# Three products of a two-layer transformer kernel moved on the tensor engine's queue

## The chip, the cores and the metric

The kernel runs on one NeuronCore of a Trainium2 chip. Its engines have a queue of instructions each and meet only through semaphores: TensorE (PE, matmuls and transposes), VectorE (DVE), ScalarE (ACT), GpSimd (POOL) and SyncE (SP, which here issues every DMA). The metric is the device time of one execution in microseconds (us). Before the change it was 1876.63 us, the median of 3 runs (1875.66 to 1876.63).

## The reference

Four sequences of 512 tokens by 256 features pass two layers. Shortened to what is computed:

```python
x = L0_attn_x                                  # (4, 512, 256)
xn = _layernorm(x)
x = x + attn(xn) + ffn0(xn)    # 16 heads of 128, causal; a binarized 256x256 product with bias
xn = _layernorm(x)
x = x + mamba2(xn) + ffn1(xn)  # 64 heads of 64 (32 pairs), state 128; a gated product of width 704

# attn, for each head: k, q, v = W_K xn, W_Q xn, W_V xn
scores = q k^T, masked, softmax;  z = attn v;  out = W_O z
# mamba2: proj = xn @ in_proj_w (a gate, x, B, C and dt), a convolution of 4 taps and silu on x, B and C,
# the state-space product in chunks, times silu(gate), an RMS norm over 4096, out_proj_w
```

## The kernel before, in words

The order of the work on each engine is written out by hand, one function per engine. `sequence(b, last)` is one of the four sequences, b = 0 to 3. It runs 16 attention heads (`head`), the end of the attention, the start of the second layer, and then 32 pairs of Mamba heads (`pair`, numbered n = 0 to 31).

Where more than plain fp32 rounding is wanted, an operand is split in a high part (ACT copies it out of PSUM as fp32r) and a low part (DVE or POOL subtracts the high one), and three matmuls are made of one (`mm3`, line 745). So a projection of queries or of keys over 256 features is 6 matmuls of 128x512, and a half of the values is 12 of 128x256.

**A head.** On PE: the queries (into bank 0) and keys (bank 1) of the next head (`project_qk`), the transposes of this head's probabilities (`turn_probs`, lines 831, 837 and 842), for even heads the second half of the values of this head and the next one (`project_v`, bank 0), the scores of the next head (`score`, from line 750), and probabilities times values (`weigh_values`). DVE takes in this order: the low parts of the next queries (line 1455) and keys (line 1426), three low parts of the turned probabilities, the low part of the values, the mask and the maxima, and `normalise` (line 1499), which divides the next head's probabilities by their sum. ACT copies the high parts in the same order: queries, keys, three of probabilities, values.

`project_v` overwrites bank 0 and so waits for `s_q_ev`, which line 1455 counts up when the queries have left it. `turn_probs` waits for `s_norm_done` from line 1499. `weigh_values` waits for `s_v_ev`, the low part of the values. The first head of the first sequence has its queries, keys, first half of values, scores and `normalise` ahead of the loop.

**A pair.** On PE: the gate of pair n+1 (`project_gate`, bank 0), the x of pair n+2 (`project_x`, bank 1), the transposes of the x of pair n+1 (`turn_x`, line 1006, which waits for the convolution's end on DVE, line 1519), the output product of pair n-1 (`project_out`, line 1047, which waits for DVE line 1687), and then `in_block` (L1034), `off_block` (L1023) and `make_states` (L1014). Pair 30 has no `project_x`, since there is no pair 32. Pair 31 makes the queries and keys of the next sequence's head 0 (`first_qk`), reading that sequence's normalised input from its own place, `xn_next`. After pair 31 come the first half of the next sequence's values (`project_v`), its first scores, `project_out` of pair 31, and a sum of squares (line 1129).

**Weights.** There are two buffers, `w_r` of parity 0 and 1. In the first sequence they are loaded, split and saved to DRAM; afterwards SP fetches the split ones. SP's queue at the end of a sequence is `next_heads(b, par)`: for parity 0 it waits until the gate of pair 30 has been made (the last reader of that buffer), and fetches head 0's query and key weights (line 415) and value weights (line 418). For parity 1 it waits for the gate of pair 31, copies `xn_next` to `xn_r` (line 435), and fetches head 1's weights. In the first sequence the saves and loads of the output weights (lines 412 and 400) stand ahead of both, and SP takes its queue strictly in order. `w_wait` is PE's wait for such a fetch (semaphore `w_fetched0` for parity 0).

Of the kernel before, what the change touches and what calls it, by code (L numbers as in the profile page):

```python
# [34 lines left out]
def two_layers(nc, x, wqkv, wo_t, w0, b0, w_pair, w_out, w_bc, w_dt, conv_par, dt_bias, a_log,  # L35
               d_col, norm_col, gate_t, up_t, down_t, gate_s, up_s, down_s, out):
    NB, S, D = x.shape
    NH = wqkv.shape[0]
# [16 lines left out]
    with ExitStack() as ctx:  # L55
# [268 lines left out]
        def first(b):  # L324

            return isinstance(b, int) and b == 0
# [410 lines left out]
        def _(pe):  # L737
# [49 lines left out]
            def project_qk(b, h, par, lows=None, src=xn_now):  # L787
                N = b * NH + h
                w_wait(b, h, par)
                pe.wait_ge(s_v_ev, N + 1 - par)  # L790
                project(bank[0][:], par, 0, lows, src).then_inc(s_q_done, 1)
                pe.wait_ge(s_k_ev, N + 1)
                project(bank[1][:], par, 1, src=src).then_inc(s_k_done, 1)
# [28 lines left out]
            def turn_probs(b, h, par):  # L822
                N = b * NH + h
                pe.wait_ge(s_norm_done, N + 1)
                if not first(b):
                    pe.wait_ge(s_ms_ready, b)
                pe.wait_ge(s_pt_a, N + 1)
                if par == 0:
                    pe.wait_ge(s_v_ev, N + 2)
                for q in range(NT):  # L830
                    ins = pe.transpose(bank[5][:, q * P:(q + 1) * P], prob[:, par, P_AT[q]:P_AT[q] + P], ident[:])  # L831
                ins.then_inc(s_turned_a, 1)
                pe.wait_ge(s_pt_b, N + 1)
                pe.wait_ge(s_y_done, b * 2 + 1)
                for k, q in ((1, 1), (1, 2), (1, 3), (3, 3)):
                    at = PT_AT[k] - PT_AT[1] + (q - k) * P
                    ins = pe.transpose(bank[6][:, at:at + P], prob[:, par, P_AT[q] + k * P:P_AT[q] + (k + 1) * P], ident[:])  # L837
                ins.then_inc(s_turned_b, 1)
                pe.wait_ge(s_z_ev, N + 1)
                pe.wait_ge(s_y_done, b * 2 + 2)  # L840
                for q in (2, 3):
                    ins = pe.transpose(bank[7][:, (q - 2) * P:(q - 1) * P], prob[:, par, P_AT[q] + 2 * P:P_AT[q] + 3 * P], ident[:])
                ins.then_inc(s_turned_c, 1)
# [148 lines left out]
            def project_x(b, n, par):  # L992
                N = b * NPAIR + n
                w_wait(b, NH + n, par)
                pe.wait_ge(s_taps_done, N + b * 2 + 2)
                project(bank[1][:], par, 1).then_inc(s_xc_done, 1)
# [51 lines left out]
                             start=begin and t % 2 == 0, stop=last, skip_group_check=True)  # L1048
                ins.then_inc(s_projected, 1)

            def first_qk(b):

                project_qk(b, 0, 0, lows=b * 2 * KT, src=xn_now if first(b) else xn_next)

            def sequence(b, last):
                def head(h, par, more):

                    if more:
                        project_qk(b, h + 1, 1 - par)
                    turn_probs(b, h, par)  # L1060
                    if par == 0:
                        project_v(b, h + 1, 1, 0)
                    if more:
                        score(b, h + 1, 1 - par)
                    weigh_values(b, h, par)
                    if more and par == 1:
                        project_v(b, h + 1, 0, 5)

                with pe.Fori(0, NH // 2 - 1) as i:
                    for par in range(2):  # L1070
                        head(i * 2 + par, par, True)
                head(NH - 2, 0, True)
                pe.wait_ge(s_late, 16 * N_LATE)

                pe.wait_ge(s_v_ev, (b + 1) * NH + 1)
                pe.wait_ge(s_z_ev, (b + 1) * NH - 1)
                out_heads(0, range(NH - 2))
                turn_probs(b, NH - 1, 1)
                pe.wait_ge(s_k_ev, (b + 1) * NH + 1)
                out_heads(1, range(NH - 2))  # L1080
                weigh_values(b, NH - 1, 1)
                attention_out(b)

                mamba_start(b, last)

                def pair(n, par, more, ahead, before=2):


                    if more:
                        project_gate(b, n + 1, 1 - par)  # L1090
                    elif not last:
                        pe.wait_ge(s_gate_ready, (b + 1) * NPAIR + 1)
                        pe.wait_ge(s_taps_done, (b + 1) * (NPAIR + 2))
                        first_qk(b + 1)
                    if ahead:
                        project_x(b, n + 2, par)
                    if more:
                        turn_x(b, n + 1, 1 - par)
                    if before == 1:
                        pe.wait_ge(s_res_ready, b + 1)  # L1100
                    if before > 0:
                        project_out(b, n - 1, 1 - par, isinstance(n, int) and n == 1, False)
                    in_block(b, n, par)
                    off_block(b, n, par)
                    if more:
                        make_states(b, n + 1, 1 - par)

                make_states(b, 0, 0)
                pair(0, 0, True, True, before=0)
                pair(1, 1, True, True, before=1)  # L1110
                with pe.Fori(1, NPAIR // 2 - 1) as i:
                    for par in range(2):
                        pair(i * 2 + par, par, True, True)
                pair(NPAIR - 2, 0, True, False)
                pair(NPAIR - 1, 1, False, False)
                if not last:
                    pe.wait_ge(s_xn_copied, (b + 1) * 64)
                    project_v(b + 1, 0, 0, 0)
                if not last:
                    pe.wait_ge(s_state_ev, (b + 1) * NPAIR + 1)  # L1120
                    score(b + 1, 0, 0)
                    pe.wait_ge(s_v_ev, (b + 1) * NH + 2)
                project_out(b, NPAIR - 1, 1, False, True)
                pe.wait_ge(s_summed, (b + 1) * (NPAIR + 1) - (1 if last else 0))
                pe.wait_ge(s_hid_ready, (b + 1) * NPAIR + 1)
                if last:
                    pe.wait_ge(s_squared, (b + 1) * NPAIR + 1)
                for t in range(NT):
                    ins = mm(bank[5][:, t:t + 1], lhsT=sumsq[:, t * P:(t + 1) * P], rhs=ones[:, 0:1], start=True, stop=not last)
                    if last:  # L1130
                        ins = mm(bank[5][:, t:t + 1], lhsT=square[:, t * P:(t + 1) * P], rhs=ones[:, 0:1], start=False, stop=True)
                ins.then_inc(s_ss_done, 1)
# [1 line left out]
            keep_busy(11)  # L1134
            turn_norm(0, range(NT), (6, 7)).then_inc(s_ln_turned, 1)
            keep_busy(8)
            first_qk(0)
            project_v(0, 0, 0, 0)
            score(0, 0, 0)
            pe.wait_ge(s_v_ev, 2)  # L1140
# [669 lines left out]
```

## Time and profile before

| | |
|---|---|
| median of 3 runs | 1876.63 us (1875.66 to 1876.63) |
| the profiled execution | 1876.75 us |
| its span | 1875.0 us |
| PE busy | 1852.3 us, 99% |
| DVE, ACT, POOL busy | 1500.1, 1237.9, 828.0 us |
| mean granted clock of TensorE | 0.999 |

The 1.75 us between span and time lie outside the recorded instructions. The span is one row of four sequences: the first head's scores begin at about 18 us, and the second, third and fourth sequences' first queries and keys at 473.87, 936.50 and 1398.50 us. In a row of a timeline, a group of instructions has its start and the busy time from there. Matmuls overlap (the next begins before the modelled end of the last), so the room that a group takes on PE is read from its start to the start of the next one, not from its busy time.

### The profile page before, as it was taken

The page shows a single profiled execution, that of the slowest core. Times are in us where ns is not written, and L with a number is a line of the kernel's source. Part 1 is how long each engine was busy: PE and PEld are TensorE (multiplying, and loading weights), DVE is VectorE, ACT ScalarE, POOL GpSimd, SP SyncE. Part 2 cuts the span into 40 slices and gives each one's busy share as a digit, 9 for nine tenths or more (in the row PEclk, how much of TensorE's full clock was granted, in tenths as well). Part 3 has the DMA queues.
Part 4 walks back from the last instruction along what each step waited for, and adds up shares of the span by engine and source line. Part 5 has one row for each costly group of instructions (what it writes and reads, how often), then busy time and mean ns, then how long its engine had stood idle before and what let it go on. Part 6 is the DMA issues. An engine that isn't in the chain of part 4 may idle for free.

```text
span 1875.0 us, 42153 instructions
## 1 busy us (share of the span) xinstructions
PE 1852.3 (99%) x12602; PEld 1574.3 (84%) x12602; DVE 1500.1 (80%) x2736; ACT 1237.9 (66%) x2867; POOL 828.0 (44%) x1005
## 2 busy tenths in 40 slices
PE   8999999999999999999999999999999999999998
PEld 7888778888888878888888887888888888788886
DVE  6886778888788468888888846988888883688886
ACT  5663489999455247888755525888865551588885
POOL 2210379998200027777710002777770000277776
PEclk9999999999999999999999999999999999999999
DMA  6330478887422125656622212656652321366663
GB/s 242 126 126 1 158 231 264 259 265 240 144 78 89 54 82 194 209 205 218 210 98 79 77 54 82 227 205 206 217 189 90 91 66 54 117 215 205 207 215 112
DMA packets 157193, 290.76 MB, mean 155 GB/s; under 512 B 12944, under 2 KB 83792, under 8 KB 157008
## 3 DMA queue, kind: packets, MB, share of 16 engines
q1 hardware_dynamic: 157136, 290.04, 46.6%
q8 instruction: 31, 0.51, 0.1%
q14 instruction: 26, 0.21, 0.0%
HBM read 248.70 MB, written 38.14 MB: 153 GB/s over the span
## 4 chain that ended last, share of the span: by engine, by line
PE 92%; DVE 3%; ACT 2%; issue 1%; POOL 1%; DMA 0%; SPq 0%; POOLq 0%; DVEq 0%; ACTq 0%
PE bank L745 40%; PE bank L1047 11%; PE bank L1034 7%; PE bank L1014 6%; PE both L745 5%; PE bank L863 4%; PE bank L1023 4%; PE bank L1006 3%; PE bank L912 2%; PE bank L831 1%; PE bank L837 1%; PE both L863 1%; PE bank L753 1%; PE bank L750 1%; PE bank L751 1%
## 5 line engine op out<-in xcount | busy, mean ns | idle before, releaser
L745 PE MATMUL bank<-xn_r,w_r 128*128 128x512 f32 x2268 | 566.6, 398 | 0.9 <-DVE xn_r L1738 0.9
L745 PEld LDWEIGHTS bank<-xn_r,w_r 128*128 128x128 f32 x2268 | 412.6, 188 | 83.6 <-issue 1.1
L1510 DVE SCALAR_TENSOR_TENSOR conv_acc<-bank,conv_sb,conv_acc 128x511 f32<-128x511 f32 (+2 forms) x408 | 304.0, 745 | 44.7 <-DVE conv_acc L1510 17.3
L605 POOL TENSOR_TENSOR rstd<-var_eps,minus_half 128x4 f32<-128x4 f32 (+2 forms) x12 | 9.7, 807 | 603.8 <-DVE var_eps L1439 603.8
L1047 PE MATMUL bank<-wo_n,place 128*128 128x256 f32 x1024 | 242.4, 380 | 2.3 <-DVE place L1687 2.3
L626 POOL TENSOR_TENSOR c_grow<-c_grow,c_t 128x768 f32<-128x768 f32 x128 | 234.0, 1828 | 22.5 <-DVE place L1519 22.5
L1159 ACT ACTIVATE place_r<-bank 128x512 fp32r<-128x512 f32 (+1 forms) x320 | 158.7, 556 | 120.6 <-PE bank L745 96.0
L1426 DVE TENSOR_TENSOR place_r<-bank,place_r 128x512 fp32r<-128x512 f32 (+1 forms) x320 | 186.3, 630 | 63.6 <-ACT place_r L1159 63.6
L1047 PEld LDWEIGHTS bank<-wo_n,place 128*128 128x128 f32 x1024 | 184.8, 190 | 22.8 <-DVE place L1687 2.7
L648 POOL TENSOR_TENSOR sumsq<-sumsq,place 128x512 f32<-128x512 f32 x127 | 162.0, 1276 | 17.0 <-ACT place L1227 17.0
L1238 ACT ACTIVATE conv_acc<-bank,conv_sb 128x512 f32<-128x512 f32 x136 | 105.7, 778 | 89.2 <-PE bank L745 85.3
L636 POOL TENSOR_TENSOR carry<-state,dec 128x128 f32<-128x128 f32 x256 | 102.5, 400 | 133.9 <-ACT state L1154 112.7
L1344 ACT ACTIVATE place<-place_r,cum_t 128x128 f32<-128x128 f32 x512 | 156.0, 389 | 0.0
L1344 ACT ACTIVATE span_b<-place_r,cum_t 128x128 f32<-128x128 f32 x512 | 155.9, 389 | 0.0
L1536 DVE TENSOR_TENSOR shared<-both,cb 128x1024 f32<-128x1024 f32 x128 | 155.4, 1214 | 0.0
L1034 PEld LDWEIGHTS bank<-shared,place 128*64 128x64 f32 x2048 | 109.2, 136 | 41.8 <-issue 41.1
L619 POOL TENSOR_TENSOR shared<-place,dec 128x384 f32<-128x384 f32 x128 | 106.5, 832 | 82.6 <-DVE place L1543 82.5
L1034 PE MATMUL bank<-shared,place 128*64 128x128 f32 x2048 | 140.1, 279 | 0.0
L745 PE MATMUL bank<-place_r 128*128 128x512 f32 (+3 forms) x768 | 133.1, 322 | 0.5
L1519 DVE SCALAR_TENSOR_TENSOR place<-bank,conv_acc 128x512 f32<-128x512 f32 x128 | 88.4, 691 | 54.6 <-ACT bank L1243 54.4
L745 PEld LDWEIGHTS bank<-place_r 128*128 128x128 f32 x768 | 120.1, 188 | 14.0 <-issue 5.5
L641 POOL TENSOR_TENSOR state<-state,carry 128x128 f32<-128x128 f32 x256 | 118.4, 462 | 20.1
(174 smaller groups left out, 3544.8 us busy)
## 6 DMA issues: line engine op xcount, KB each, us to landing
place_r<-cum_rows SPq DMA_DIRECT2D x128, 512.0 KB, 4.3
c_grow<-grow_rows SPq DMA_DIRECT2D x128, 384.0 KB, 3.5
w_r<-pair_split SPq DMA_DIRECT2D x96, 512.0 KB, 3.7
w_r<-qkv_split SPq DMA_DIRECT2D x48, 512.0 KB, 4.0
pair_split<-w_r SPq DMA_DIRECT2D x32, 512.0 KB, 3.4
qkv_split<-w_r SPq DMA_DIRECT2D x16, 768.0 KB, 3.9
w_r<-qkv_split SPq DMA_DIRECT2D x48, 256.0 KB, 3.2
wo_n<-out_split SPq DMA_DIRECT2D x96, 128.0 KB, 2.0
```

Source lines behind the costliest of these rows:

```text
L626: pool.tensor_tensor(c_grow[:, par, :, :], c_grow[:, par, :, :], c_t[:, P:W].unsqueeze(1).to_broadcast([P, 2, W - P]), ALU.mult).then_inc( ...
L641: pool.tensor_tensor(state[:, c, :], state[:, c, :], carry[:], ALU.add).then_inc(s_carried, 1)
L648: pool.tensor_tensor(sumsq[:], sumsq[:], square, ALU.add).then_inc(s_summed, 1)
L745: ins = mm(out, lhsT=w(a), rhs=m(b), start=(start and i == 0), stop=(stop and i == 2), **kw)
L1014: ins = mm(bank[2][:, c * P:(c + 1) * P], lhsT=b_sb[:, c, :], rhs=x_w[:, c, :], start=True, stop=True)
L1034: ins = mm(bank[5][h * HD:(h + 1) * HD, c * P:(c + 1) * P], lhsT=x_dt[:, par, c, h * HD:(h + 1) * HD], rhs=mix[:, par, h, c * P:(c + 1) * ...
L1047: ins = mm(out_tile((6, 7), t), lhsT=hid[:, t * P:(t + 1) * P], rhs=wo_n[:, par, :], start=begin and t % 2 == 0, stop=last, skip_group_che ...
L1159: A(dst, src, ACT.Copy).then_inc(done, 1)
L1344: ins = A(span[par][:, h, c * P:(c + 1) * P], spread[:, par, h * W + c * P:h * W + (c + 1) * P], ACT.Relu, bias=cum_t[:, c, bass.ds(n * 2 ...
L1426: tt(dst, src, high.bitcast(F32), ALU.subtract).then_inc(done, 1)
L1510: stt(out=conv_acc[:, back:W], in0=src[:, 0:W - back], scalar=conv_sb[:, ch, TAPS - 1 - back:TAPS - back], in1=conv_acc[:, back:W], op0=AL ...
L1536: tt(mix[:, par, :, :], both[:].rearrange("p (h w) -> p h w", h=2), cb[:].rearrange("p t i -> p (t i)").unsqueeze(1).to_broadcast([P, 2, W ...
```

## The change

On PE alone, at three places; no other engine's program is touched. In the first sequence's head 0, `project_v` stands ahead of `turn_probs`. At the end of sequences 0 to 2, `first_qk` is taken apart: the keys (`first_k`, with the waits for the weights, for `xn_next` and for bank 1) go to pair 30, to where `project_x` stands in other pairs, and the queries (`first_q`) stay in pair 31. And heads 0 and 1 of every sequence are written out ahead of the loop over heads, which begins at head 2.

```diff
-            def first_qk(b):
-
-                project_qk(b, 0, 0, lows=b * 2 * KT, src=xn_now if first(b) else xn_next)
+            def first_q(b):
+                pe.wait_ge(s_v_ev, b * NH + 1)
+                project(bank[0][:], 0, 0, src=xn_next).then_inc(s_q_done, 1)
+
+            def first_k(b):
+                w_wait(b, 0, 0)
+                pe.wait_ge(s_k_ev, b * NH + 1)
+                project(bank[1][:], 0, 1, b * 2 * KT, xn_next).then_inc(s_k_done, 1)
 
             def sequence(b, last):
-                def head(h, par, more):
+                def head(h, par, more, begin=False):
 
                     if more:
                         project_qk(b, h + 1, 1 - par)
+                    if begin:
+                        project_v(b, h + 1, 1, 0)
                     turn_probs(b, h, par)
-                    if par == 0:
+                    if par == 0 and not begin:
                         project_v(b, h + 1, 1, 0)
...
-                with pe.Fori(0, NH // 2 - 1) as i:
+                for h in range(2):
+                    head(h, h, True, begin=first(b) and h == 0)
+                with pe.Fori(1, NH // 2 - 1) as i:
...
                         pe.wait_ge(s_gate_ready, (b + 1) * NPAIR + 1)
-                        pe.wait_ge(s_taps_done, (b + 1) * (NPAIR + 2))
-                        first_qk(b + 1)
+                        first_q(b + 1)
                     if ahead:
                         project_x(b, n + 2, par)
+                    elif more and not last:
+                        pe.wait_ge(s_taps_done, (b + 1) * (NPAIR + 2))
+                        first_k(b + 1)
...
-            first_qk(0)
+            project_qk(0, 0, 0, lows=0)
```

PE's queue in the first sequence's head 0, before (`place_r,w_r` and `xn_r,w_r` are products of the input with query or key weights, `w_r,xn_r` is half of the values, `ident,place` are transposes; a loop's entry comes first):

```order
L1069 UNCONDITIONAL_BRANCH [waits v_ev]
L1069 ISA
L790 REGISTER_ALU [waits w_ready]
L745 MATMUL bank<-xn_r,w_r 128x512 [waits v_ev]
L745 MATMUL bank<-xn_r,w_r 128x512 x5
L792 REGISTER_ALU
L745 MATMUL bank<-xn_r,w_r 128x512 [waits k_ev]
L745 MATMUL bank<-xn_r,w_r 128x512 x5
L831 MATMUL bank<-ident,place 128x128 [waits v_ev,pt_a,norm_done]
```

The same place after the change:

```order
L745 MATMUL bank<-xn_r,w_r 128x512 [waits v_ev,w_ready]
L745 MATMUL bank<-xn_r,w_r 128x512 x5
L745 MATMUL bank<-xn_r,w_r 128x512 [waits k_ev]
L745 MATMUL bank<-xn_r,w_r 128x512 x5
L745 MATMUL bank<-w_r,xn_r 128x256 [waits q_ev,w_ready]
L745 MATMUL bank<-w_r,xn_r 128x256 x11
L831 MATMUL bank<-ident,place 128x128 [waits v_ev,pt_a,norm_done]
```

The twelve matmuls of the values, with their wait for `q_ev`, have come ahead of the transposes and their wait for `norm_done`.

PE's queue in pair 30 and at the head of pair 31 of the first sequence, before:

```order
L745 MATMUL bank<-xn_r,w_r 128x512 [waits gate_ready]
L745 MATMUL bank<-xn_r,w_r 128x512 x5
L1006 MATMUL bank<-ident,place 128x128 [waits conv_silu]
...
L1014 MATMUL bank<-shared,b_sb 128x128 x2
L745 MATMUL bank<-place_r,w_r 128x512 [waits v_ev,w_fetched0,xn_lo,taps_done,gate_ready]
L745 MATMUL bank<-place_r,w_r 128x512 x2
L745 MATMUL bank<-place_r,w_r 128x512 [waits xn_lo]
L745 MATMUL bank<-place_r,w_r 128x512 x2
L745 MATMUL bank<-place_r,w_r 128x512 [waits k_ev]
L745 MATMUL bank<-place_r,w_r 128x512 x5
```

The same place after the change:

```order
L745 MATMUL bank<-xn_r,w_r 128x512 [waits gate_ready]
L745 MATMUL bank<-xn_r,w_r 128x512 x5
L745 MATMUL bank<-place_r,w_r 128x512 [waits k_ev,xn_lo,w_fetched0,taps_done]
L745 MATMUL bank<-place_r,w_r 128x512 x2
L745 MATMUL bank<-place_r,w_r 128x512 [waits xn_lo]
L745 MATMUL bank<-place_r,w_r 128x512 x2
L1006 MATMUL bank<-ident,place 128x128 [waits conv_silu]
...
L1014 MATMUL bank<-shared,b_sb 128x128 x2
L745 MATMUL bank<-place_r,w_r 128x512 [waits v_ev,gate_ready]
L745 MATMUL bank<-place_r,w_r 128x512 x5
```

Six matmuls, and with them the waits for `w_fetched0` and `taps_done`, have moved from behind pair 30's work to right behind the gate of pair 31.

## Rows read from the trace of the kernel before

**Rows 1.** The page: busy time of each engine.
```profile
PE 1852.3 (99%) x12602; PEld 1574.3 (84%) x12602; DVE 1500.1 (80%) x2736; ACT 1237.9 (66%) x2867; POOL 828.0 (44%) x1005
```
**Rows 2.** Waits of PE: total us, times, longest us.
```profile
PE bank L1006 <- DVE place L1519: 2.3, 5, 0.5
```
**Rows 3.** Timeline of PE, first heads: start us, busy us, group, idle before.
```profile
19.85 2.95 PE L745 MATMUL bank<-xn_r,w_r 128*128 128x512 f32 x12
24.51 0.66 PE L831 MATMUL bank<-ident,place 128*128 128x128 f32 x4 [1.72 <-DVE place L1499]
...
25.58 1.67 PE L745 MATMUL bank<-w_r,xn_r 128*128 128x256 f32 x12
27.09 0.40 PE L750 MATMUL bank<-place_r 128*128 128x512 f32 x1
...
29.02 2.04 PE L745 MATMUL bank<-place_r 128*128 128x512 f32 x12
...
33.71 0.63 PE L831 MATMUL bank<-ident,place 128*128 128x128 f32 x4
```
**Rows 4.** Timeline of DVE, the same stretch.
```profile
23.18 1.27 DVE L1499 TENSOR_SCALAR place<-place,inv_total 128x128 f32<-128x128 f32 x4
24.37 0.68 DVE L1455 SCALAR_TENSOR_TENSOR place_r<-bank,place_r 128x512 fp32r<-128x512 f32 x1
...
25.89 1.62 DVE L1426 TENSOR_TENSOR place_r<-bank,place_r 128x512 fp32r<-128x512 f32 x3 [0.24 <-ACT place_r L1159]
27.92 0.69 DVE L1426 TENSOR_TENSOR place_r<-bank,place_r 128x512 fp32r<-128x512 f32 x1 [0.41 <-ACT place_r L1159]
...
32.35 1.27 DVE L1499 TENSOR_SCALAR place<-place,inv_total 128x128 f32<-128x128 f32 x4
```
**Rows 5.** Timeline of PE, end of the first sequence.
```profile
466.48 1.64 PE L745 MATMUL bank<-xn_r,w_r 128*128 128x512 f32 x6
468.67 0.65 PE L1006 MATMUL bank<-ident,place 128*128 128x128 f32 x4 [0.55 <-DVE place L1519]
...
473.87 3.03 PE L745 MATMUL bank<-place_r,w_r 128*128 128x512 f32 x12 [0.27 <-issue]
476.74 1.89 PE L1047 MATMUL bank<-wo_n,place 128*128 128x256 f32 x8
...
480.94 1.67 PE L745 MATMUL bank<-w_r,xn_r 128*128 128x256 f32 x12 [0.64 <-DMA w_r<-qkv_split]
```
**Rows 6.** SP's queue there; and DMA issues of 467.3 to 468: KB, us to landing.
```profile
467.46 0.63 SPq L415 DMA_DIRECT2D w_r<-qkv_split  x1
...
w_r<-qkv_split SPq DMA_DIRECT2D x1, 512.0 KB, 6.2
```
**Rows 7.** Timeline of PE, end of the second sequence.
```profile
929.62 1.64 PE L745 MATMUL bank<-xn_r,w_r 128*128 128x512 f32 x6
931.81 0.66 PE L1006 MATMUL bank<-ident,place 128*128 128x128 f32 x4 [0.55 <-DVE place L1519]
...
939.40 1.89 PE L1047 MATMUL bank<-wo_n,place 128*128 128x256 f32 x8
...
942.89 1.70 PE L745 MATMUL bank<-w_r,xn_r 128*128 128x256 f32 x12
```
**Rows 8.** Timeline of DVE, the same stretch.
```profile
936.72 0.69 DVE L1687 TENSOR_TENSOR place<-bank,place 128x512 f32<-128x512 f32 x1
```
**Rows 9.** DMA issues of 923.7 to 924.4: KB, us to landing.
```profile
w_r<-qkv_split SPq DMA_DIRECT2D x1, 512.0 KB, 3.9
```
**Rows 10.** Timeline of PE's start; two stretches behind its last matmul (PEclk third from right).
```profile
3.57 4.65 PE L759 MATMUL both<-upto,ident 128*128 128x128 f32 x22 [3.57 <-POOL causal_bf L599]
...
10.44 1.95 PE L759 MATMUL both<-upto,ident 128*128 128x128 f32 x16
...
1869.41:1871.68 2.27, 0.00 (x0) 0.00 (x0) 1.04 (x4) 0.00 (x0) 1.02 (x1) 0.92 0.00 0
...
1871.40:1873.00 1.60, 0.00 (x0) 0.00 (x0) 1.06 (x3) 0.00 (x0) 0.00 (x0) 0.50 0.23 84
```

## The prediction

> **What bounds the kernel.** I read the page's busy times first: PE is busy 99% of the span [rows 1], so a change on PE's queue can give back only the idle time it removes, and every wait it adds is paid in full unless a later wait of PE shrinks by it. Next the waits of PE over the whole run. The one that the moved keys aim at comes 5 times with 2.3 us in total, once in pair 30 of each sequence [rows 2]. Then the timelines of PE, DVE and SP at the two places of the change, to see what each moved instruction waits for at its new place. About 0.2% (3.75 us) is what a measurement of this kernel can tell from no change.
>
> **Term A, the first head.** Before, PE has issued the queries and keys of head 1 by about 22.8 (19.85 + 2.95) and stands still until 24.51, when `normalise` (23.18 + 1.27 = 24.45) lets the transposes go [rows 3, 4]. The values are put in front of that wait. But they overwrite bank 0, and wait for the queries to leave it, and that is line 1455, which stands behind `normalise` in DVE's queue and ends at 24.37 + 0.68 = 25.05 [rows 4]. So the values cannot begin before about 25.15: the wait becomes longer by 0.6 us instead of being filled. From there:
> - The values take 27.09 - 25.58 = 1.51 us of PE [rows 3] and end at 26.7. The transposes, which began at 24.51, begin at 26.7, 2.2 later.
> - DVE's three low parts of the probabilities began 1.38 behind the transposes (25.89 against 24.51) and its low part of the values ended 2.72 behind that beginning (27.92 + 0.69 = 28.61) [rows 3, 4]. ACT and DVE take the probabilities first and then the values, so the early values gain nothing there; with no pause between them (the two idles of 0.24 and 0.41 in rows 4 mostly go) the four take about 2.2, and end near 26.7 + 1.38 + 2.2 = 30.25. Before it was 28.61: 1.65 later.
> - `weigh_values` needs that last one. It began at 29.02 without a wait [rows 3] and will begin at about 30.35. The mask, maxima, exponentials and second `normalise` hang on DVE's queue in the same way: that one ended at 32.35 + 1.27 = 33.62, and PE's transposes began at 33.71 with 0.09 to spare [rows 3, 4]. At 33.62 + 1.65 = 35.27 it releases them at 35.3.
> That is +1.6 us at 33.71. From there PE has no wait behind which it could hide. The bounds: +0.6 if only the wait for bank 0 is paid and the ones behind it vanish, +2.2 if the whole shift of the transposes stays. I take +1.6, since the row of the second `normalise` sets it.
>
> **Term B, the end of the first sequence.** The gate of pair 31 begins at 466.48. Twelve matmuls of this shape take 476.74 - 473.87 = 2.87 us of PE, so six take 1.43, and PE is free at 467.9 [rows 5]. Before, it stood until the transposes at 468.67. Now the keys come here, and with them the wait for head 0's weights. SP issues that fetch at 467.46, and it lands 6.2 us later, at 473.66 [rows 6]. Before, the first product that read it began at 473.87 [rows 5], right behind that landing; it was already late there, since from the transposes to that product it took 5.20 us here (473.87 - 468.67) and 4.72 in the second sequence (939.40 - 2.87 - 931.81) [rows 5, 7]. SP cannot issue it sooner: nothing on SP depends on the moved matmuls, and what stands ahead of it is unchanged. So PE waits with `turn_x`, `project_out`, `in_block`, `off_block` and `make_states` of pair 30 queued behind the keys, from 467.9 to 473.87.
> - `turn_x` begins at 473.87 + 1.43 = 475.3. From `turn_x` to the values of the next sequence the second sequence took 942.89 - 931.81 = 11.08 us [rows 7], of which 1.43, the keys, are now ahead: 9.65. The values begin at 484.95.
> - Before they began at 480.94, which holds a wait of 0.64 for head 1's weights [rows 5]; that wait is gone in the shift.
> B = +4.0 us. Bounds: the same fetch took 3.9 us at the second sequence [rows 9], which would put the keys at about 471.5 and B at +1.6; if it came as much later again as it here came behind that one (2.3 us), B would be +6.3. I take the landing of this very fetch.
>
> **Term C, the ends of the second and third sequences.** There nothing is saved or loaded by SP ahead of the fetch, it is issued before 924.4 and lands 3.9 us later [rows 9], well before PE needs it at 929.62 + 1.43 = 931.05 [rows 7]. The keys fill the gap until 931.81: `turn_x` begins at 932.48, 0.67 late, and the queries alone follow in pair 31, so `project_out` comes at 939.40 + 0.67 - 1.43 = 938.64. It needs line 1687, which ended at 937.41 and moves to 938.1 [rows 7, 8], so this wait does not come up. The gain is 0.76 each, -1.5 for two. Bounds 0 (a new wait of the same size) and -1.7.
>
> **Term D, the clock.** The longest wait of PE at the two places before is 1.72 us [rows 3], and the clock was full all along. Under this change it stands 6 us in B. The row that shows what this does is at the end: in the 2.27 us behind the last matmul the mean granted clock is 0.92, and from 1871.40 on it is 0.50 [rows 10], the lower of the two levels, 1.2 GHz against 2.4. So it fell after about 1.9 us of standing still (0.92 means 0.36 us of the 2.27 at half). At the start, PE's first 22 small matmuls took 4.65 us, 211 ns each, and 16 of the same a little later 1.95, 122 each [rows 10]; the difference over the 22 is 2.0 us. I take this as the price of one climb back after the 6 us: D = +2.0. Bounds 0 (the clock stays) and +4.0 (twice that).
> The Trainium skill, "TensorE: Matmul & The Clock Gate", section "HAM oscillation — how this bites in real kernels", says that a DMA wait between groups of matmuls can drop the clock, so that the next group starts at the lower one. The rows at the end of the span agree with it in kind; by this rule D is paid, and without it the sum is 2.0 less.
>
> **The two heads written out** (some 180 queue rows more) I cost at nothing: the stretch between the loops is already written out so, and PE has no wait for instructions there. The loop's edge costs nothing visible either. Bound: 0.5 us for a sequence, the size of the longest wait of rows 2.
>
> **Sum.** 1.6 + 4.0 - 1.5 + 2.0 = +6.1 on the span of 1875.0 is 1881.1; with the 1.75 outside it 1882.85. The profiled execution (1876.75) is 0.1 above the median (1876.63), so the forecast is 1882.7.
>
> **The rivals.**
> 1. *The clock stays up or recovers at once.* For it: the row at the end has small products ahead of the pause, where here large ones stand, and may not carry over. Against it: 6 us is three times the 1.9 after which it fell. D = 0: 1880.7. Chance 25%.
> 2. *The fetch lands sooner than in the trace before.* For it: 3.9 us at the second sequence [rows 9]. Against it: SP and the DMA traffic up to the landing are unchanged. B = 1.6 and a pause of 3.6 us; without D the sum is +1.7, 1878.4. Chance 10%. The Trainium skill, "DMA: Bandwidth & Descriptors", section "Anatomy of one DMA — SWDGE (gpsimd) path", gives about 2.0 us plus bytes over 436 GB/s for a DMA; for 512 KB that is an estimate of 3.2 us, against 6.2 measured here on another issuing path. By the page PE would stand some 3 us less in B.
> 3. *The keys are covered in all three ends, and the kernel is faster.* Place: the landing of that one fetch. The values would begin no later than before if it landed by 469.6 (480.94 - 9.65 - 1.43 and 0.2 for the start), 2.1 us after its issue; every tenth below is a gain. If it were there at 467.9, B would be -0.76 for the gap, -0.5 for the late start of 473.87 and -0.64 for the values' wait, -1.9, and the sum 1.6 - 1.9 - 1.5 = -1.8: 1874.8; with the queries out of bank 0 in time as well, A is about -1.5 and the time 1871.7. Against it stand both landings of rows 6 and 9. Chance 3%.
> 4. *It costs more*: the fetch lands later in the contended stretch, the clock takes two climbs, or the written-out heads cost instruction fetches. One of these at its bound gives about 1885. Chance 12%.
>
> The forecast keeps 50%. The range 1879.0 to 1885.5 takes in the rival without D, the forecast, and most of rival 4; some of 2 and 3 lie below. More than 0.2% slower is above 1880.4: the forecast, rival 4 and somewhat over half of rival 1, 0.76. Within 0.2%: the rest of rival 1 and rival 2, 0.20. Faster: 0.04.
>
> **What would show it.** In the profile after: the values of head 1 start at about 25.15, released by DVE L1455, and the second head's transposes near 35.3. One wait of PE near 6 us at 468 plus 1.6, released by the DMA `w_r<-qkv_split`; behind it matmuls of 512 columns at a longer spacing and a granted clock of 0.50 for some 4 us. In the next two ends no wait at L1006. If SP's fetch lands before 470, or the values start before 24.5, a step here is wrong.

## The result and the profile after

The change makes the kernel slower: 1885.68 us, the median of 5 runs (1882.13 to 1886.56), against 1876.62 us, the median of 5 runs of the kernel before (1875.66 to 1876.63). The ratio is 1.0047, with a 95% interval of 1.0032 to 1.0062. The forecast was 1882.7 in a range of 1879.0 to 1885.5 us, so the direction and the two waits hold, and the size was too small by 3 us: by the median the time is 0.2 us above the range's upper end, by the ratio (1.0047 on 1876.63 is 1885.45) right at it. It lies where the fourth rival, with a chance of 12%, had put it (about 1885). One execution in all the experiments, of the kernel of experiment 8, took 2295.31 us at a mean granted clock of 0.752, and no comparison here uses it.

The page and the waits of PE of the changed kernel (total us, times, longest us) answer to [rows 1, 2]:

```profile
PE 1856.7 (99%) x12602; PEld 1578.4 (84%) x12602; DVE 1499.7 (80%) x2736; ACT 1238.4 (66%) x2867; POOL 828.9 (44%) x1005
```

```profile
PE bank L745 <- issue: 5.9, 1, 5.9
...
PE bank L745 <- DVE place_r L1466: 3.0, 4, 2.4
...
PE bank L1006 <- DVE place L1530: 0.7, 2, 0.5
```

The same number of instructions keeps PE busy 4.4 us longer, which waits alone can't do. There is one wait of 5.9 us and one of 2.4, and the wait for the convolution's end has gone from 5 times to 2. The timeline of PE at the first head answers to [rows 3]:

```profile
20.41 2.92 PE L745 MATMUL bank<-xn_r,w_r 128*128 128x512 f32 x12
25.77 2.67 PE L745 MATMUL bank<-w_r,xn_r 128*128 128x256 f32 x12 [2.43 <-DVE place_r L1466]
28.24 1.05 PE L831 MATMUL bank<-ident,place 128*128 128x128 f32 x4
...
32.39 2.11 PE L745 MATMUL bank<-place_r 128*128 128x512 f32 x12 [0.38 <-DVE place_r L1437]
...
37.32 0.66 PE L831 MATMUL bank<-ident,place 128*128 128x128 f32 x4
```

The values wait for the queries' low part (line 1466 now), as forecast. But they then take 2.47 us of PE (28.24 - 25.77) where they took 1.51, and the transposes 1.05 where they took 0.66. The end of the first sequence answers to [rows 5]:

```profile
470.10 1.64 PE L745 MATMUL bank<-xn_r,w_r 128*128 128x512 f32 x6
477.60 2.90 PE L745 MATMUL bank<-place_r,w_r 128*128 128x512 f32 x6 [5.85 <-issue]
480.29 1.06 PE L1006 MATMUL bank<-ident,place 128*128 128x128 f32 x4
481.14 3.02 PE L1047 MATMUL bank<-wo_n,place 128*128 128x256 f32 x8
...
491.46 1.69 PE L745 MATMUL bank<-w_r,xn_r 128*128 128x256 f32 x12
```

Six matmuls of 512 columns take 2.69 us of PE (480.29 - 477.60) instead of 1.43, and the output product 2.95 (the next group began at 484.09) instead of 1.82. The stretches of both places (us, PE, PEld, DVE, ACT and POOL busy, granted clock, DMA share, GB/s) show why:

```profile
26.03:29.44 3.41, 3.41 (x18) 3.41 (x18) 0.19 (x1) 0.05 (x1) 1.44 (x1) 0.50 0.54 216
```

```profile
470.00:476.60 6.60, 1.75 (x10) 1.13 (x8) 3.39 (x5) 3.72 (x7) 2.94 (x5) 1.00 0.82 245
476.60:483.40 6.80, 5.80 (x16) 4.73 (x17) 0.69 (x1) 0.00 (x0) 1.24 (x2) 0.50 0.72 263
483.40:488.00 4.60, 4.60 (x45) 3.79 (x44) 2.08 (x3) 1.09 (x2) 1.97 (x3) 1.00 0.00 0
```

The granted clock was 0.50 (1.2 GHz) in both places, and not in the second one alone. The clock was still full until 476.60, about 4.9 us into the long wait. That wait is put down to "issue", which names no releaser; SP's queue in the changed kernel shows the fetch, issued 6.5 us before the keys began, and the list of DMA issues (KB, us to landing) shows it landing after 6.4:

```profile
470.55 0.43 SPq L400 DMA_DIRECT2D raw_out<-in_w_out  x1
471.09 0.63 SPq L415 DMA_DIRECT2D w_r<-qkv_split  x1
```

```profile
w_r<-qkv_split SPq DMA_DIRECT2D x1, 512.0 KB, 6.4
```

The end of the second sequence answers to [rows 7]:

```profile
940.16 1.64 PE L745 MATMUL bank<-xn_r,w_r 128*128 128x512 f32 x6
941.63 1.56 PE L745 MATMUL bank<-place_r,w_r 128*128 128x512 f32 x6
943.03 0.60 PE L1006 MATMUL bank<-ident,place 128*128 128x128 f32 x4
...
952.63 1.70 PE L745 MATMUL bank<-w_r,xn_r 128*128 128x256 f32 x12
```

Here nothing waits: from the gate to the values it is 12.47 us against 13.27 before (942.89 - 929.62), 0.80 less.

Measured from fixed points, the 8.9 us between the two spans (1883.9 and 1875.0) are all found:

| place | from start to start | before | after | difference |
|---|---|---|---|---|
| up to head 1's queries | 0 to PE L745 | 19.85 | 20.41 | +0.56 |
| first head | that to head 1's transposes | 13.86 | 16.91 | +3.05 |
| end of sequence 0 | gate of pair 31 to the values | 14.46 | 21.36 | +6.90 |
| end of sequence 1 | the same | 13.27 | 12.47 | -0.80 |
| end of sequence 2 | the same | 13.26 | 12.48 | -0.78 |

These are one profiled execution of each kernel, and not all of them are alike. Of the five executions of the changed kernel four took 1884.88 us or more, at mean granted clocks of 0.995 and 0.996, and one 1882.13 us, at 0.998. And the 14.46 us before, at the end of sequence 0, hold late starts that differ from execution to execution (experiments 4 and 7).

### The profile page after: what moved, and what is told of

Read it like the earlier page. It is cut to its first block, busy times and chain, and to the rows that moved or that the text cites. A ratio compares the mean times of both kernels' runs of the same rounds, so it can differ in the third digit from the quotient of the medians.

```text
span 1883.9 us, 42124 instructions
## 1 busy us (share of the span) xinstructions
PE 1856.7 (99%) x12602; PEld 1578.4 (84%) x12602; DVE 1499.7 (80%) x2736; ACT 1238.4 (66%) x2867; POOL 828.9 (44%) x1005
## 4 chain that ended last, share of the span: by engine, by line
PE 93%; DVE 3%; ACT 2%; issue 2%; POOL 1%; POOLq 0%; DVEq 0%; ACTq 0%
PE bank L745 40%; PE bank L1047 12%; PE bank L1034 7%; PE bank L1014 6%; PE both L745 5%; PE bank L863 4%; PE bank L1023 4%; PE bank L1006 3%; PE bank L912 2%; PE bank L831 2%; PE bank L837 1%; PE both L863 1%; PE bank L753 1%; PE bank L750 1%; PE bank L751 1%
## 5 line engine op out<-in xcount | busy, mean ns | idle before, releaser
L745 PE MATMUL bank<-xn_r,w_r 128*128 128x512 f32 x2268 | 566.5, 398 | 0.9 <-DVE xn_r L1749 0.9
L745 PEld LDWEIGHTS bank<-xn_r,w_r 128*128 128x128 f32 x2268 | 412.6, 188 | 83.6 <-issue 1.1
L745 PE MATMUL bank<-place_r 128*128 128x512 f32 (+3 forms) x768 | 133.2, 322 | 0.8 <-DVE place_r L1437 0.4
L745 PEld LDWEIGHTS bank<-place_r 128*128 128x128 f32 x768 | 120.0, 188 | 14.7 <-issue 5.9
```

The lines of the kernel that those rows point to most:

```text
L745: ins = mm(out, lhsT=w(a), rhs=m(b), start=(start and i == 0), stop=(stop and i == 2), **kw)
```

## The experiments

All are variants of the kernel before. "Places" are the stretches of the table above. The kernels were timed beside the kernel before on the same chips, whose median was 1876.29, 1875.91 and 1876.21 us in the three groups (experiments 1 to 4, 5 to 8 and 9 to 12).

**1. The first head's values alone**, with the two heads of every sequence written out as in the change.

```diff
+                    if begin:
+                        project_v(b, h + 1, 1, 0)
                     turn_probs(b, h, par)
-                    if par == 0:
+                    if par == 0 and not begin:
```

> Only the first head's values are put in front of its transposes (with the two heads written out); the keys of the next sequences stay where they were. Theory: the wait for bank 0 and what hangs on it costs 1.6 us, and the clock falling once during the 2.4 us wait costs another 1.5, so +3.1 us in the profile where the clock falls, +1.6 where it doesn't, and nothing at the ends of the sequences. Rival: the extra came from the written-out heads, spread over the four sequences; then more than +3.1, and the first head alone shows about +1.6.

1880.06 us, ratio 1.002 (1.0011 to 1.0029). The first head's place is 2.3 us longer (37.27 - 21.09 = 16.18), between the two figures, with the same wait of 2.43 us; the clock fell here later than in the changed kernel, when the values were done, and hit the transposes and scores:

```profile
21.09 2.92 PE L745 MATMUL bank<-xn_r,w_r 128*128 128x512 f32 x12
26.45 1.67 PE L745 MATMUL bank<-w_r,xn_r 128*128 128x256 f32 x12 [2.43 <-DVE place_r L1459]
27.95 1.02 PE L831 MATMUL bank<-ident,place 128*128 128x128 f32 x4
28.76 1.06 PE L837 MATMUL bank<-ident,place 128*128 128x128 f32 x4
...
37.27 0.60 PE L831 MATMUL bank<-ident,place 128*128 128x128 f32 x4
```

```profile
28.00:31.30 3.30, 3.30 (x14) 3.04 (x13) 1.50 (x3) 2.04 (x5) 0.16 (x1) 0.50 0.03 9
```

Another 1.24 us of its profile lie ahead of 21.09, where the changed kernel was at 20.41 and the kernel before at 19.85; in this profile the clock also fell once at about 11 us, among the first products. The end of the first sequence, where nothing was edited, is 0.48 shorter (484.07 - 470.09 = 13.98), and the three add up to the 3.1 between the spans. By the medians it is +3.8. So neither of the two theories has it whole: the first head costs 2.3 to 3.1, and something else is lost at the start.

**2. The keys at the end of the first sequence alone.** `first_k` and `first_q` as in the change, for that end only; the others keep `first_qk`.

```diff
+                        if b in (0,):
+                            first_q(b + 1)
+                        else:
                             first_qk(b + 1)
                     if ahead:
                         project_x(b, n + 2, par)
+                    elif more and b in (0,):
+                        first_k(b + 1)
```

> Only the keys at the end of the first sequence are moved to pair 30. Theory: the wait for the weights' landing costs 4.0 us and the low clock behind it 2.8, so +6.8 us, a wait of PE of about 5.9 us at 468 and a granted clock of 0.50 for some 5 to 7 us there. Rival: the low clock hides behind work that waits anyway; then about +4.0.

1883.76 us, +7.5 by the medians, ratio 1.0042 (1.0028 to 1.0056), and +6.5 in the profile's place (487.50 - 466.55 = 20.95), near the +6.8 of the theory:

```profile
466.55 1.64 PE L745 MATMUL bank<-xn_r,w_r 128*128 128x512 f32 x6
473.56 2.90 PE L745 MATMUL bank<-place_r,w_r 128*128 128x512 f32 x6 [5.37 <-issue]
...
487.50 1.69 PE L745 MATMUL bank<-w_r,xn_r 128*128 128x256 f32 x12
```

That is the larger part of the whole loss, and the low clock isn't hidden.

**3. The keys at the ends of the second and third sequences alone.** The same edit with `b in (1, 2)`.

> Only the keys at the ends of the second and third sequences are moved. Theory: each fills a gap of 0.76 us and waits for nothing new, so -1.5 to -1.6 us, a time of about 1875.1. Rival: the gap comes back later (the maxima or the sum of squares), and the time stays at 1876.6.

1874.72 us, ratio 0.9992 (0.9983 to 1.0001): -1.57 by the medians, with an interval that just reaches no change; -1.5 by the profile's spans. The wait at line 1006 is left in the first and last sequence alone. The gain is given back nowhere.

**4. The two heads written out alone.**

```diff
-                with pe.Fori(0, NH // 2 - 1) as i:
+                for h in range(2):
+                    head(h, h, True)
+                with pe.Fori(1, NH // 2 - 1) as i:
```

> Heads 0 and 1 of every sequence are written out ahead of PE's loop, the order of all work is that of before. Theory: 0 (within 0.2 us). Rival: instruction fetches of the longer program cost up to 0.5 us a sequence, +2 us.

1877.18 us, +0.9 by the medians, ratio 1.0005 (0.9996 to 1.0014): by itself inconclusive. The profile shows no wait in or between the heads, but head 1's queries begin at 20.45 instead of 19.85. The load of x, issued at 1.36 us in both, lands later, and VectorE's first work waits for it. DMA issues of the first microseconds (KB, us to landing), of before and of this kernel:

```profile
x_sb<-in_x SPq DMA_DIRECT2D x1, 512.0 KB, 3.5
```

```profile
x_sb<-in_x SPq DMA_DIRECT2D x1, 512.0 KB, 4.1
```

Over all fourteen profiles of this study the eight with PE's heads written out show 4.1 to 4.4 us, five of the other six 3.4 to 3.5 and the sixth 3.9. Where no slow products come between, head 1's queries follow the landing: they begin at 19.68 to 19.85 with a landing of 3.4 or 3.5 us, at 20.41 and 20.45 with 4.1, and at 20.60 to 20.63 with 4.3.

By its span (1874.5) this kernel is 0.5 shorter than the kernel before, although it begins later. That lies at the end of the first sequence, where nothing was edited: the late fetch landed here 5.5 us after its issue, in time, and the place is 480.46 - 467.20 = 13.26 us instead of 14.46:

```profile
467.20 1.64 PE L745 MATMUL bank<-xn_r,w_r 128*128 128x512 f32 x6
...
474.07 3.06 PE L745 MATMUL bank<-place_r,w_r 128*128 128x512 f32 x12
...
480.46 1.70 PE L745 MATMUL bank<-w_r,xn_r 128*128 128x256 f32 x12
```

**5. The long waits filled with matmuls of no use.** On the changed kernel:

```diff
                     if begin:
+                        for _ in range(9):
+                            mm(bank[5][:, 0:P], lhsT=ident[:], rhs=upto[:], start=True, stop=True)
                         project_v(b, h + 1, 1, 0)
...
             def first_k(b):
+                if b == 1:
+                    for _ in range(22):
+                        mm(bank[1][:, 0:P], lhsT=ident[:], rhs=upto[:], start=True, stop=True)
                 w_wait(b, 0, 0)
```

> The changed kernel, with matmuls of no use put into its two long waits: 9 small products (ident times upto into bank 5) ahead of the first head's values, 22 (into bank 1) ahead of the wait for the weights at the end of the first sequence. The outputs stay those of the reference. Theory: the waits stay (values at about 25.2 to 25.8, keys at 6.2 us behind the fetch), but the clock doesn't fall in either, and of the +8.9 us about 4.3 go: +4.1 to +4.6 against before. Rival: the clock isn't what the 4.3 us are; then the time stays at +8.9.

1881.54 us (7 runs), ratio 1.0029 (1.0018 to 1.004): 31 more products, each of two passes, and less time than the changed kernel, 3.4 us by the medians (+5.6 against +9.1 over the kernel before) and 4.4 by the spans (1879.5 and 1883.9), where the theory had 4.3. The granted clock is 1.00 in both places:

```profile
470.26 5.07 PE L1062 MATMUL bank<-upto,ident 128*128 128x128 f32 x44
476.17 1.66 PE L745 MATMUL bank<-place_r,w_r 128*128 128x512 f32 x6 [0.84 <-DMA w_r<-qkv_split]
477.67 0.60 PE L1006 MATMUL bank<-ident,place 128*128 128x128 f32 x4
```

```profile
476.00:483.00 7.00, 6.83 (x55) 5.76 (x56) 1.93 (x3) 0.42 (x1) 2.61 (x2) 1.00 0.59 213
```

The end of the first sequence is now 487.28 - 468.78 = 18.50 us, +4.04, and the first head 36.10 - 20.62 = 15.48, +1.62: the two waits alone, as the prediction's terms B and A had them. What the changed kernel has above that, 2.86 and 1.43, is the clock. With the PE kept busy the profile also names the releaser of the long wait, the DMA of the weights. By the medians this kernel is +5.6 and by the spans +4.5; most of what is between them is that the profiled execution of before (1876.75) lies 0.8 above the median of before in this group (1875.91).

**6. The keys at all three ends, and the fetch issued sooner.** No values moved, no heads written out; on SP, in the first sequence:

```diff
-                for n in range(NPAIR - 4, NPAIR):
+                for n in range(NPAIR - 4, NPAIR - 2):
                     pair(n, n % 2, n + 1 < NPAIR, n + 2 < NPAIR, False)
-                for par in range(2):
-                    sp.wait_ge(w_saved[par], SLOTS * 8)
-                    next_heads(0, par)
+                pair(NPAIR - 2, 0, False, False, False)
+                sp.wait_ge(w_saved[0], SLOTS * 8)
+                next_heads(0, 0)
+                grow_load(0, NPAIR - 1, 1)
+                pair(NPAIR - 1, 1, False, False, False)
+                sp.wait_ge(w_saved[1], SLOTS * 8)
+                next_heads(0, 1)
```

> The keys are moved at all three ends, the first head is that of before, and in the first sequence SP issues head 0's fetch right when the gate of pair 30 is done, ahead of the load of c_grow for pair 31 and of pair 31's output weights. Theory: the wait of 5.9 us was that fetch standing behind other entries of SP's queue; issued at about 462 it lands before 468, PE doesn't wait at the keys, and the end of the first sequence gains as well: -0.8 for the gap, -0.5 for the late start of the queries, up to -0.6 for the wait for head 1's values, with the other two ends -2.9 to -3.4 us in all, about 1873.5. Rival: the fetch is slow because of the traffic at this place and lands late wherever it is issued, or the loads moved behind it come late themselves (off_block of pair 31, the output product of pair 31); then +1 us or more against before.

1872.86 us, ratio 0.9985 (0.9976 to 0.9994): 3.05 us below the kernel before, inside the expected 2.9 to 3.4. SP's queue and PE's timeline:

```profile
460.70 0.63 SPq L415 DMA_DIRECT2D w_r<-qkv_split  x1
461.37 0.61 SPq L418 DMA_DIRECT2D w_r<-qkv_split  x1
465.72 0.39 SPq L453 DMA_DIRECT2D c_grow<-grow_rows  x1
```

```profile
466.30 1.64 PE L749 MATMUL bank<-xn_r,w_r 128*128 128x512 f32 x6
467.77 1.56 PE L749 MATMUL bank<-place_r,w_r 128*128 128x512 f32 x6
...
478.78 1.70 PE L749 MATMUL bank<-w_r,xn_r 128*128 128x256 f32 x12
```

The fetch is issued at 460.70, took 5.1 us, and is there 2 us before the keys. The place is 12.48 us, -1.98, where the change had made it +6.90. Seen from the start of pair 31's gate, the fetch is issued 5.6 us ahead of it instead of 1.0 behind it, and takes 5.1 us instead of 6.4. With the 6.4 it would still land at 467.1, before the keys. So the stall came from its place in SP's queue, behind the wait for `off_block` of pair 29 and the output weights. Of the -1.98, 1.2 are the late starts that this place had before.

**7. The early fetch alone**, on the kernel before.

> The kernel before with SP's early fetch alone. Theory: the queries and keys of the second sequence begin at once behind pair 30 instead of 0.5 us late, and the wait of 0.64 for head 1's values may go: -0.5 to -1.1 us. Rival: no difference, since the values' wait grows by what the queries gain.

1875.29 us, ratio 0.9997 (0.9988 to 1.0006): -0.6 by the medians, not told from nothing. The place is 480.76 - 467.49 = 13.27, -1.19: both late starts are gone. One profile doesn't show that the early fetch did this, since experiment 4 had the same 13.26 without it. But in the four profiles with the late fetch and the keys of this end unmoved (before and experiments 1, 3 and 4) the place takes 13.26 to 14.68 us, and in the six with the early fetch and the keys moved always 12.47 or 12.48. In the profiled execution the gain is made up for ahead of the place, where the clock fell in the first 15 us (queries of head 1 at 20.77):

```profile
7.20:10.50 3.30, 1.35 (x12) 1.16 (x12) 1.54 (x5) 0.00 (x0) 1.56 (x2) 1.00 0.58 184
10.60:13.90 3.30, 3.30 (x17) 3.30 (x16) 1.38 (x3) 2.37 (x3) 1.17 (x1) 0.50 1.13 374
```

**8. The changed kernel with the early fetch.** The edit of experiment 6 on SP.

> The changed kernel with SP's early fetch. Theory: the end of the first sequence turns from +6.9 to about -1.9, the first head keeps its +1.6 and, where the clock falls in it, +1.5 more: between -1.8 and +0.2 us against before. Rival: as in the kernel without the first head's change, the fetch is late anyway; then +4 or more.

1876.76 us, the median of ten executions, ratio 1.0003 (0.9994 to 1.0013). By the medians that is +0.85, above the expected -1.8 to +0.2; the theory had left out the 0.9 of the written-out heads. By the span of the profile (1873.4) it is -1.6. The rival (+4 or more) falls. The executions come in two groups, four at 1875.2 to 1875.6 us with mean granted clocks of 0.998 and 0.999, and six at 1876.5 to 1877.6 us with 0.997 and 0.998. In the profile, of the first group, the clock stays up through the first head, and that head's place is 15.48, +1.62, without any filling:

```profile
26.00:30.00 4.00, 4.00 (x31) 3.87 (x31) 1.61 (x3) 1.81 (x5) 1.70 (x1) 1.00 0.39 157
```

**9. The queries out of bank 0 sooner.** On experiment 6, with the first head's values first (and so PE's heads written out), and on DVE the first two heads written out as well, so that the low part of head 1's queries stands ahead of the first division:

```diff
             maxima(0, 0, 0)
+            q_low(1)
             normalise(0, 0, 0)
```

> Keys moved at all three ends with SP's early fetch, the first head's values in front of its transposes, and DVE takes the low part of head 1's queries (which frees bank 0) ahead of the first division of the probabilities instead of behind it. Theory: the first head's loss was bank 0 waiting behind that division on DVE, and then the values' low part behind the probabilities'. The first goes: the values begin about 1.5 us behind the queries and keys instead of 2.4 to 2.5 (the first step takes a wait of about 0.9 us out), the second stays, so the first head costs about 0.6 to 0.7 us instead of 1.6, and the clock doesn't fall. Rival: the values were held by something else (the weights, ScalarE's copy), and they begin as late as before: 1.6.

1874.92 us, ratio 0.9993 (0.9984 to 1.0002), 0.8 above the same kernel with no values moved (experiment 10). The wait ahead of the values is shorter by 0.9, the next one stays, and the place is 35.82 - 21.25 = 14.57, +0.71:

```profile
21.25 2.92 PE L749 MATMUL bank<-xn_r,w_r 128*128 128x512 f32 x12
25.69 1.67 PE L749 MATMUL bank<-w_r,xn_r 128*128 128x256 f32 x12 [1.52 <-DVE place_r L1477]
...
30.89 2.11 PE L749 MATMUL bank<-place_r 128*128 128x512 f32 x12 [0.52 <-DVE place_r L1449]
...
35.82 0.66 PE L835 MATMUL bank<-ident,place 128*128 128x128 f32 x4
```

Both steps of the first head's term stand as they were written: DVE's order holds the values, and then DVE's order holds `weigh_values`.

**10 and 11. Experiment 6 with the two heads written out, and experiment 6 once more.**

> Keys moved at all three ends with SP's early fetch, and the two heads of every sequence written out ahead of PE's loop. Theory: the same time as without them (1872.9), the 0.9 us seen alone being the scatter of the first 15 us. Rival: the longer program costs 0.5 to 1 us.

> Keys moved at all three ends with SP's early fetch, once more beside the three others on the same chip. Theory: 3 us below the kernel before, as in the first run of it. Rival: the first was luck of the chip, and the gain is under 1.5 us.

1874.13 us (1873.64 to 1875.78, 11 runs) and 1873.24 us (1873.02 to 1874.04, 11 runs), ratios 0.999 (0.9981 to 1.0) and 0.9985 (0.9976 to 0.9994). The gain of experiment 6 is there again, -3.0. The written-out heads cost 0.9 by the medians, the same as in experiment 4, and the theory that this was scatter falls. The first head's place is 13.86 in both experiment 10 and the kernel before; the loss is all ahead of it (21.18 against 19.83 for head 1's queries, of which some is a fall of the clock at 11 us in this profile).

**12. The values first, with the wait filled.** Experiment 6 with the first head's part of experiment 5.

> Keys moved at all three ends with SP's early fetch, the first head's values in front of its transposes, and 9 products of no use (ident times upto into bank 5) in the wait ahead of them. The outputs stay those of the reference. Theory: the first head costs 1.6 us in every run and the clock doesn't fall in it, so +1.6 over the kernel with the early fetch and no values moved, with a small scatter, where the unfilled one had two groups of times 1.5 to 2 us apart. Rival: the scatter isn't the clock's, and both groups stay.

1875.74 us (1875.09 to 1876.92), ratio 0.9998 (0.9989 to 1.0007). The place is 36.07 - 20.60 = 15.47, +1.61, at full clock. By the medians it is 1.6 above experiment 10, which has the same written-out heads and no values moved, and 2.5 above experiment 11. Ten of its eleven executions lie within 1.0 us and the eleventh 0.8 above them, all with a mean granted clock of 0.998 or 0.999: the second group of experiment 8 is gone.

## Why the prediction was right, and where its size was off

- **Term A, the waits of the first head** (+1.6): measured 1.61 and 1.62 at full clock in experiments 5, 8 and 12. Its steps hold as well: in experiment 5, less its 0.77 us of later start, the transposes begin at 26.71, `weigh_values` at 30.40 and head 1's transposes at 35.33, where the forecast had 26.7, 30.35 and 35.3. Taking its first step away left 0.71 (experiment 9).
- **Term B, the wait for the weights** (+4.0): measured 4.04 at full clock (experiment 5), and turned into -1.98 by an earlier place of the fetch in SP's queue (experiment 6). Both are counted from the one profile before, whose place holds 1.2 us of late starts that another execution hasn't got (experiment 4), so the size is good to about 1 us only, and its agreement to 0.04 is partly luck. The third rival's figure for this place if the fetch were there in time was -1.9.
- **Term C** (-1.5): measured -0.80 and -0.78 in the changed kernel, and -1.5 in experiment 3.
- **Term D, the clock** (+2.0): this term was mis-sized. It measured 2.86 at the end of the first sequence, since the clock stayed at 0.50 for 6.8 us, 5.8 of them with PE busy, and not for the some 4 us that the prediction took from the start of the kernel. That row was a doubtful measure: the granted clock reads 1.00 while those 22 slow products run, so the trace doesn't show that the lower clock slowed them. A stretch in the middle of them (us, busy times, granted clock third from right):

```profile
3.50:6.00 2.50, 2.43 (x11) 2.43 (x12) 1.09 (x4) 0.12 (x1) 0.01 (x1) 1.00 1.05 355
```

  The term also had a second place that the prediction didn't see: 1.43 in the first head, behind a wait of 2.43 us. The prediction compared the 6 us of term B with the 1.9 us after which the clock had fallen at the end of the span [rows 10], and should have held the 2.4 us of term A against them too. Together 4.3 instead of 2.0. Nor is 1.9 us a limit: in the long wait the clock fell only after about 4.9 us.
- **The written-out heads** (0, bound 0.5 a sequence): +0.56 in the changed kernel's profile and 0.9 by two pairs of medians. The reason given for nothing, that PE has no wait for instructions in such stretches, holds; the cost sits at another place, in the landing of the first load. Why that load is later with a longer program on PE is not shown by any run here.

With these the sum is 0.56 + 3.05 + 6.90 - 1.58 = 8.93 instead of 6.1. A slip that changes nothing: of the 5 waits at line 1006 [rows 2] four are those of pair 30, and the fifth, of 0.2 us, comes at the start of the first sequence's pairs.

What came is the fourth rival in two of its three parts, the clock falling at two places and a price for the written-out heads. The third part, a fetch that lands later, didn't come, and the heads' price is in the first load and not in instruction fetches between the products. The range had been drawn to take in most of that rival; that the time lies at its end and not clearly beyond is owed to that, not to the sum.

The first rival (clock stays up) falls for the long wait; for the first head it is what some executions do, as the profile of experiment 8 shows (that its two groups of times are this fits with their mean granted clocks and with experiment 12, but only one execution was profiled). The second and third (the fetch lands sooner) fell, since it landed as in the trace before, 6.4 us after its issue against 6.2. The Trainium skill, "DMA: Bandwidth & Descriptors", section "Anatomy of one DMA — SWDGE (gpsimd) path", gives a fit for DMAs issued by GpSimd, by which 512 KB would be there in an estimated 3.2 us; this one is issued by SP, and it took 4.7 to 6.5 us in this stretch in the fourteen profiles, and the measurement decides.

## What to carry to other kernels

Before work is moved into a gap, list what it waits for at its new place, and look up on the releasing engine or queue what stands ahead of the release: here both moved pieces were held by queue order, on DVE and on SP, not by a duration, and moving one DMA issue turned a loss of 6.9 us into a gain of 2.0. Look at the same untouched stretch in more than one profile before a tenth of a microsecond is read from it: this one differed by 1.4 us with nothing edited in it. A wait of TensorE can have a second price behind it, the lower clock: 2.86 us behind the wait of 5.9, and 1.43 behind the one of 2.4; hold every new wait against the shortest pause after which the trace shows the clock to fall, not only the longest wait, and give it a chance and not a certainty, since the same wait of 2.43 us had a fall behind it in two profiles and none in a third. The version with all three ends moved, the fetch early, and neither the first head nor the loop touched is the one to keep: 1872.9 and 1873.2 us.

## What the runs showed of the hardware that was not expected

- The granted clock fell around a wait of 2.43 us of a TensorE that was otherwise busy with large products, in the changed kernel and experiment 1, and didn't fall in the profiles of experiments 5 and 12 (wait filled) and 8 (not filled). In experiment 1 it fell some 1.5 us after the wait was over. Waits of 1.71 to 1.74 us at the same place had no fall behind them in any of the eight profiles without the values moved. In the long wait of the changed kernel it fell after about 4.9 us, at the end of the span after 1.9 [rows 10]: no one length of pause goes with the fall in these traces.
- In the profiles of experiments 1, 7 and 10 it fell at about 11 us, behind the wait for the normalised input ahead of the kernel's first transposes. That wait was 2.09, 1.95 and 2.03 us there, and 0.7 to 1.8 in the eleven profiles whose granted clock stays at 1.00; with a landing of 3.4 or 3.5 us it took 0.7 to 1.5, with 3.9 or more 1.4 to 2.1. Head 1's queries began 0.5 to 1.1 us later than in profiles of the same sort without the fall, in experiment 7 in part because its load landed later. The line is that of experiment 10:

```profile
10.34 1.17 PE L770 MATMUL bank<-ident,xn 128*128 128x128 f32 x8 [2.03 <-DVE xn L1466]
```

  The Trainium skill, "TensorE: Matmul & The Clock Gate", section "HAM oscillation — how this bites in real kernels", warns of waits for a DMA between groups of products; here a wait for VectorE had the same effect. In experiment 9 the same products ran as slowly although the granted clock reads 1.00 there, as it does over the first products of the kernel before; why is open.
- The first load of the kernel took 4.1 to 4.4 us to land in all eight profiles with the longer PE program, and 3.4 to 3.9 in the six others. The reason is open.
